# A transformer layer on eight cores: the order and the queues of the weight loads in the stage that quantizes the feed-forward weights

## The reference

```python
# attention, 16 heads of 64, causal
q, k, v = (heads(ln(x) @ W.T + b) for W, b in ((Wq, bq), (Wk, bk), (Wv, bv)))
a = softmax(causal(q @ k.T / 8)) @ v
x = x + ln(a @ Wo.T + bo)
# feed-forward layer with three-valued weights
def quantize(W):
    gamma = mean(abs(W))
    return clip(round(W / (gamma + 1e-5)), -1, 1)
h = relu(ln(x) @ quantize(W1).T + b1)        # 1024 -> 4096
x = x + ln(h @ quantize(W2).T + b2)          # 4096 -> 1024
```

## Time and profile before

| what | us |
|---|---|
| median of 6 runs | 3279.53 |
| lowest and highest run | 3274.54, 3388.69 |
| the profiled execution, its own time | 3277.28 |
| its span on the slowest core (core 1) | 3275.7 |
| spans of the 8 cores | 3263.8 to 3275.7 |
| PE busy | 2617.9 (80%) |
| ACT busy | 1864.3 (57%) |
| DVE busy | 992.2 (30%) |
| POOL busy | 114.1 (3%) |
| mean granted TensorE clock | 0.910 |

### The profile page before, as it was taken

One profiled execution on the slowest core, in us unless ns is written; L12 is line 12 of the kernel. 1 busy time (PEld: TensorE's weight loads), 2 busy tenths in 40 slices (PEclk: granted clock), 3 DMA queues, 4 the chain that ended last, 5 costly groups with the idle time before them and its releaser, 6 DMA issues.

```text
span 3275.7 us, 42129 instructions; the slowest of 8 cores (3263.8 to 3275.7 us)
## 1 busy us (share of the span) xinstructions
PE 2617.9 (80%) x14120; PEld 1166.5 (36%) x14120; DVE 992.2 (30%) x1704; ACT 1864.3 (57%) x2679; POOL 114.1 (3%) x189
## 2 busy tenths in 40 slices
PE   2466787787988778888988881079999999999997
PEld 0222232231322233322322220045566555565554
DVE  1665444232220254432321004922221222212221
ACT  2135666767789556777788993534344443444432
POOL 0010000000000000000000000000000000000000
PEclk9978888887999889989999995589999999999999
DMA  6333112112010011110000006711111111111100
GB/s 104 103 116 90 40 50 81 41 45 77 8 30 4 18 47 33 31 33 6 29 17 4 6 4 173 264 46 39 43 49 33 33 40 43 49 33 33 39 27 20
DMA packets 47489, 162.24 MB, mean 50 GB/s; under 512 B 6192, under 2 KB 6320, under 8 KB 45232
## 3 DMA queue, kind: packets, MB, share of 16 engines
q0 software_dynamic: 23520, 83.91, 9.3%
q1 hardware_dynamic: 23760, 75.63, 7.3%
HBM read 142.75 MB, written 25.17 MB: 51 GB/s over the span
## 4 chain that ended last, share of the span: by engine, by line
PE 58%; ACT 17%; issue 9%; DVE 8%; DMA 7%; ACTq 1%; DVEq 0%; POOL 0%; POOLq 0%; PEldq 0%; SPq 0%
ACT s_PT L514 10%; PE pSA L825 7%; PE pSB L825 7%; PE pSC L851 7%; PE pSD L851 7%; PE pSA L479 5%; PE pSB L479 3%; PE pBA L503 3%; PE pBB L503 3%; DMA s_gbuf<-w2T 2%; ACT s_PT L521 2%; DMA s_gbuf<-w1Tp 2%; PE pBA L776 2%; PE pSD L447 2%; PE pSD L429 2%
## 5 line engine op out<-in xcount | busy, mean ns | idle before, releaser
L514 ACT ACTIVATE s_PT<-pBA,s_cneg 128x1024 bf16<-128x1024 f32 x512 | 581.8, 1136 | 261.1 <-PE pBA L503 260.7
L514 ACT ACTIVATE s_PT<-pBB,s_cneg 128x1024 bf16<-128x1024 f32 x448 | 509.6, 1137 | 14.4 <-PE pBB L503 14.3
L503 PE MATMUL pBA<-s_QT,s_KT 64*128 64x512 bf16 x1152 | 242.7, 412 | 248.2 <-ACT s_PT L514 232.0
L479 PE MATMUL pSA<-s_PT,s_V 128*128 128x512 bf16 x960 | 403.2, 420 | 19.2 <-DVE s_PT L531 17.4
L479 PE MATMUL pSB<-s_PT,s_V 128*128 128x512 bf16 x960 | 398.2, 415 | 0.1
L531 DVE TENSOR_TENSOR s_PT<-s_PT,s_tri 128x256 bf16<-128x256 bf16 x256 | 74.0, 291 | 668.2 <-ACT s_PT L514 561.4
L825 PE MATMUL pSA<-s_ln3T,s_w1qT 128*128 128x256 bf16 x2048 | 266.3, 273 | 4.6 <-ACT s_ln3T L813 4.6
L825 PE MATMUL pSB<-s_ln3T,s_w1qT 128*128 128x256 bf16 x2048 | 265.9, 273 | 0.0
L503 PE MATMUL pBB<-s_QT,s_KT 64*128 64x512 bf16 x1152 | 243.0, 414 | 23.0 <-ACT s_PT L521 5.0
L503 PEld LDWEIGHTS pBA<-s_QT,s_KT 64*128 64x128 bf16 x1152 | 65.8, 94 | 494.9 <-issue 489.7
L728 ACT ACTIVATE s_rstdd<-s_st2d,s_eps 128x1 f32<-128x1 f32 x96 | 27.6, 288 | 376.4 <-DVE s_st2d L726 376.4
(11 more groups left out here) (145 smaller groups left out, 2956.1 us busy)
## 6 DMA issues: line engine op xcount, KB each, us to landing
s_xb<-x SPq DMA_DIRECT2D x64, 512.0 KB, 4.2
s_gbuf<-w1Tp POOLq DMA_DIRECT2D x32, 512.0 KB, 5.2
s_gbuf<-w2T POOLq DMA_DIRECT2D x32, 512.0 KB, 4.8
s_wst<-w2T SPq DMA_DIRECT2D x32, 512.0 KB, 5.3
s_wst<-w1Tp POOLq DMA_DIRECT2D x16, 1024.0 KB, 6.9
s_xb<-x POOLq DMA_DIRECT2D x32, 512.0 KB, 3.9
y<-s_outst SPq DMA_DIRECT2D x32, 512.0 KB, 3.0
OTS<-s_OTst POOLq DMA_DIRECT2D x64, 128.0 KB, 2.4
```

The lines of the kernel that those rows point to most:

```text
L479: par=par, c=c: e.matmul(pOT[:, 0:512], vsl, s_PT[bb][:, par * 512:(par + 1) * 512], start=(c == 0), stop=(c == nchunks - 1)),
L503: qb=qb: e.matmul(pST[:, par * 512:(par + 1) * 512], s_KT[par * 64: par * 64 + 64, pr * T + c * 128: pr * T + (c + 1) * 128], s_QT[qb][par ...
L514: S.add("ac", lambda e, pST=pST, bb=bb, pg=pg: e.activation(s_PT[bb][:], pST[:], AF.Exp, bias=s_cneg[:, 48 + pg:49 + pg], scale=0.125), re ...
```

## The change

There are five edits:

1. `s_otr` is allocated ahead of the loop, and its first two loads are issued by SP right behind the barrier `cd`, no longer behind `cd2`. To make room, `s_cneg` (used in attention only) moves to the memory that is freed after attention, and `s_m2` is no buffer of its own any more.
2. `s_m2` becomes another name of `s_sg`, and the waits of `quant_w2` name it ("sg",). ACT's write of the next step's signs must now wait until DVE has subtracted.
3. The load of `s_woT` is issued by POOL behind the whole loop, no longer ahead of it.
4. The 32 loads of W2 go from SP to POOL.
5. The calls `otr_load(0)` and `otr_load(1)` behind `cd2` go away, as they are edit 1 now.

```diff
@@
-        dma("gp", s_woT[:].rearrange("p (c d) -> p c d", c=DC),
-            d_woT.rearrange("(c p) d -> p c d", p=128), "wo", writes=[("wo",)])
+        s_otr = [cd.enter_context(nc.sbuf_tensor(f"s_otr{i}", [128, 1024],
+                                                 BF16))
+                 for i in range(4)]
+        for t0 in range(2):
+            S.add("sp", lambda e, t0=t0: e.dma_start(
+                s_otr[t0][:].rearrange("p (a s) -> p a s", a=8),
+                d_ots[:, t0, :, :]),
+                reads=[("OTS", pair, 0) for pair in range(8)],
+                writes=[("otr", t0)], dma="otr%d" % t0)
@@
-        s_m2 = cq.enter_context(nc.sbuf_tensor("s_m2", [128, 2048], BF16))
+        s_m2 = s_sg
@@ def quant_w2(step, dst):
-                S.add("sp", lambda e, src=src, b=b, j=j: e.dma_start(
+                S.add("gp", lambda e, src=src, b=b, j=j: e.dma_start(
                     s_wst[b][:, j * 1024:(j + 1) * 1024], src),
                     writes=[("wst", b)], dma="wst%d" % b)
@@
                 s_m2[:], s_wst[b][:], s_gs[:, 1:2], -0.5, ALU.mult, ALU.is_lt),
-                reads=[("wst", b), ("gs",)], writes=[("m2",)])
+                reads=[("wst", b), ("gs",)], writes=[("sg",)])
             S.add("dv", lambda e, dst=dst: e.tensor_sub(
                 dst, s_p2[:], s_m2[:]),
-                reads=[("p2",), ("m2",)], writes=[("w2q",)])
+                reads=[("p2",), ("sg",)], writes=[("w2q",)])
@@ after the loop of 16 steps
+        dma("gp", s_woT[:].rearrange("p (c d) -> p c d", c=DC),
+            d_woT.rearrange("(c p) d -> p c d", p=128), "wo", writes=[("wo",)])
         cq.close()
         S.barrier("cd2")
@@
-        otr_load(0)
-        otr_load(1)
```

More of the change, by code:

```diff
@@ L191, in build_program @@
         s_eps = st.enter_context(nc.sbuf_tensor("s_eps", [128, 1], F32))
-        s_cneg = st.enter_context(nc.sbuf_tensor("s_cneg", [128, 80], F32))
         s_gs = st.enter_context(nc.sbuf_tensor("s_gs", [128, 2], F32))
@@ L215, in build_program @@
         ps = contextlib.ExitStack()
+        s_cneg = ps.enter_context(nc.sbuf_tensor("s_cneg", [128, 80], F32))
         s_wqT = ps.enter_context(nc.sbuf_tensor("s_wqT", [128, DC * D], BF16))
@@ L709, in build_program @@
                    for i in range(1)]
-        s_otr = [cd.enter_context(nc.sbuf_tensor(f"s_otr{i}", [128, 1024], BF16))
-                 for i in range(4)]
         s_st12d = [cd.enter_context(nc.sbuf_tensor(f"s_st12d{i}", [128, 12], F32))
```

## The result

The changed kernel is slower: 1.0126 times the kernel before, with a 95% interval of 1.0108 to 1.0144, about 41 us. I had forecast no change that could be measured (3281 us, range 3270 to 3299). Many executions of the changed kernel, the profiled one too, had one die at a lower granted clock: the ratio leaves these out, the two timed runs that are left took 3319.42 and 3320.46 us against a median of 3279.61 us before (10 runs), and I read the profile on core 5, which is on the other die.

What follows compares the result with a forecast made beforehand. DVE was taken to bound the loop, transfers close behind. Some 21 us gained at the head and 5 behind the barrier, against 20 given back in the loop plus uncovered `s_woT`, made 3281 us, range 3270 to 3299.

Steps and rivals of the forecast that it cites:

- W2 on POOL's queue: Stage 2 loop: the second W2 half waits for the first, next loads queue behind; 8.6 us a step for 7.26.
- the shared buffer: Stage 2 loop: ACT's next sign waits for DVE's subtraction; a step of about 8.2 us for 7.26, hidden at 8.6.
- the bound of 9.95: Upper limit for one stage 2 round: 0.55 issue, 6.8 loaded W1 landing and 2.6 us more.
- The ring: Stage 2 loads on POOL: 0.55 us to issue, then 2 MB landing before the next round; 8.6 us a round.
- Rival A: Stage 2 loop: second W2 half's wait on POOL makes rounds slower than 8.96 us, kernel 3294 to 3301; chance 0.29.
- The head: Start of stage 2: first W1 load no longer waits behind the `s_woT` load; about 21 to 22 us gained.
- `s_woT` at the end: End of stage 2: its load lands about 12.3 us behind the last W2 half, 3.8 us of it covered.
- the `s_otr` wait: Behind the barrier after stage 2: PE no longer waits for this load, issued early; 4.87 us gained.
- rival B: Stage 2 loop: loads run ahead, DVE and ACT set a pace of 8.2 us, kernel 3270 us; chance 0.20.

Runs made afterwards that it cites:

- own_m2: The changed kernel with `s_m2` a buffer of its own again (two of four `s_otr` buffers allocated behind the loop): 3313.25 us, 10.52 us a step.
- compare_tt: The changed kernel with DVE's W1 comparison made by tensor_tensor against a broadcast 0.5 instead of tensor_scalar: 3286.85 us, beside 3279.66 for the kernel before.

## Why the prediction was wrong

The failed step is the one headed "W2 on POOL's queue". The mechanism was right: a ring through the wait of the second half set the pace, and the shared buffer vanished beside it (own_m2). The size was wrong: 10.46 us a round, mean of 8 cores, for 8.6, outside even the bound of 9.95 that I gave. Of its two terms, the 0.55 us from a landing to the next issue was right (0.54). The one that failed is the landing of the 2 MB that go out together, 7.85 from the rows and 8.05 in the 8.6: from the issue of the second half to the landing of the next first half it measured 9.90 us in the changed kernel, and 8.15 in compare_tt, where the issues are not held. Here is the sum, from the end of attention, each term as the mean of 8 cores in the changed kernel:

| term, us | forecast | changed kernel | compare_tt |
|---|---|---|---|
| last attention work to first W1 landed | 10.2 | 10.9 | 11.6 |
| to the landing of the first second half | 16.2 | 16.7 | 17.6 |
| one round | 8.6 | 10.46 | 8.71 |
| last half to `s_woT` landed | 12.3 | 12.6 | 12.1 |
| to PE's first product with it | 0.95 | 1.66 | 1.66 |
| sum, 15 rounds | 158.4 | 187.9 | 162.0 |

- **The ring.** The rows that I built it from had POOL's issues outside a ring and none of them held, so they gave the ring without the hold-up. For that case they were right within 0.1 us (8.65 and 8.71 measured). The missing 1.86 us times 15 is 27.9 of the 29.5 us between the two sums. The bound failed because W1 landed after 8.2 us (median of each core, then the mean), not after 6.8; its 2.6 for the second MB is in no row either, rows 5 and 6 give 2.45.
- **Rival A** was the case that came, with the mechanism named and priced too low: I allowed one comparison, 1.2 us, at most, and gave the whole rival a chance of 0.29. What I read as no evidence ("the trace neither bears it out nor excludes it") was a W1 issue that started well inside a comparison and showed 0.53 us. That row could not have shown a hold: the issue ended at 2039.15, 0.12 us behind the comparison, just where the held ones end too. It was so throughout: on the 8 cores before, 103 of 128 W1 issues overlapped a comparison, all started 0.81 us or more into it, and none was longer than 0.54 us. The ring moved the start to 0.10 to 0.48 us.
- **The head** gained 19.2 us on the mean core for 21 to 22 (34.1 to 14.9). I had read the head before on core 1, where it was the longest of the eight, 36.5 us.
- **`s_woT` at the end** was right within 0.3 us. So was the loss of the `s_otr` wait: PE's first product follows its bias product without one.
- **The baseline.** I set the forecast of 158.4 us against core 1, the slowest, whose stage 2 was 157.2 us. The mean core had 152.7, and that is what a kernel whose cores do the same work moves by. Against it, my own sum would have said 5.7 us slower, near the 7.2 us that compare_tt shows in its one pair of runs. That error alone would have left the time inside the range.
- **Two slips** that changed nothing: sixteen steps of 7.26 us are 116 us, and the rest of the 119 is the start of the first; and step 13 of rival B comes at 2101.7, not at 2101.4.

Of the 41 us that the kernel lost, stage 2 explains 35 on the mean core. Stage 3 explains none: from PE's first product with `s_woT` it took 1137 to 1139 us on six cores of the changed kernel and 1137 to 1138 before. The spans of the three executions of 3319.03, 3319.42 and 3320.46 us show where most of the rest is: their mean core took 3306 us, 37 more than the 3269 of the profiled execution before, and their slowest core, which the metric counts, stood 12 us above that mean, for 7 before. A ring whose step differs between the cores (10.0 to 10.7 us) would do that; it is not shown.

## What to carry to other kernels

Before you move a DMA to another engine's list, write down what stands behind each wait there: a wait that cost nothing on a list of its own becomes the pace of the loop when the next step's loads queue behind it. If the list is GpSimd's, look for VectorE tensor_scalar work that the same landings start, since a ring can lock the two together. Compare a stage on the mean core, not on the slowest one.

## What the hardware showed that I had not expected

- A GpSimd DMA issue that started 0.10 to 0.48 us into a VectorE tensor_scalar of 1.23 us took 0.86 to 1.25 us in place of 0.53, and ended 0.12 us behind it. One that started 0.81 us in took 0.53 and showed nothing. A tensor_tensor of 2.29 us at the same place left it at 0.53.
- In a ring with such a held issue a round of 2 MB took 1.8 us longer, though the hold itself was 0.67 us. One execution in which all eight cores had the hold and only four the longer round shows that the one can pass without the other.
- The same 2 MB ring, with every comparison running, took 8.12 us a round from SyncE's queue in the middle of the stage. SyncE's next issue came 0.07 us behind a landing, GpSimd's 0.54.
